# Linear attention and feed-forward in one kernel: rows in three half-batch slots, two normalisations on other engines, another order at the passage, and the state sums' bank for attended products

## What is computed

```python
q, k, v = x @ Wq.T + bq, x @ Wk.T + bk, x @ Wv.T + bv      # split in 16 heads of 16
q = softmax(q, axis=-1);  k = softmax(k, axis=-2)          # k over the rows
state = einsum('bhnd,bhne->bhde', k, v)
out = einsum('bhnd,bhde->bhne', q, state)
out = layer_norm(out) * ln_g + ln_b
x = layer_norm(x + out @ Wo.T + bo)                         # attention layer
h = gelu(layer_norm1(x) @ ternary(w1).T + b1)               # 1024 hidden
x = layer_norm(x + layer_norm2(h) @ ternary(w2).T + b2)     # feed-forward layer
```

## Time and profile before

| | us |
|---|---|
| median of 3 runs | 558.14 (557.33 to 558.61) |
| profiled execution | 558.38 |
| its span, first to last instruction | 556.4 |
| TensorE busy in the span | 533.2 (96%) |
| VectorE, ScalarE, GpSimd busy | 481.3, 481.7, 405.7 |
| TensorE's mean granted clock | 0.992 |

### The profile page before, as it was taken

The page is one execution under the profiler, slowest core; times in us unless marked ns, Lnnn a source line. Parts: engine busy times, 40 slices in busy tenths (PEclk is TensorE's granted clock), DMA queues, the critical chain, the costliest instruction groups (busy, mean ns, idle before and its releaser), DMA issues. The chain is left out here.

```text
span 556.4 us, 10878 instructions
## 1 busy us (share of the span) xinstructions
PE 533.2 (96%) x3533; PEld 490.5 (88%) x3533; DVE 481.3 (86%) x1230; ACT 481.7 (87%) x955; POOL 405.7 (73%) x420
## 2 busy tenths in 40 slices
PE   8999999999999999989899999999999999999991
PEld 7999999898999989779788998999999999999890
DVE  5878998989899898948687899999999999999895
ACT  5746798798979878778889999999999999999993
POOL 3965979877787977476558876876776776676693
PEclk9999999999999999999999999999999999999996
DMA  8530050411605030241111022222012222110012
GB/s 340 201 113 0 4 226 2 173 56 69 234 1 228 1 115 39 75 155 75 76 40 33 13 71 77 77 76 68 39 50 77 77 77 77 45 34 38 39 39 113
DMA packets 12679, 46.51 MB, mean 84 GB/s; under 512 B 1360, under 2 KB 3792, under 8 KB 10448
## 3 DMA queue, kind: packets, MB, share of 16 engines
q1 hardware_dynamic: 12336, 45.28, 22.6%
q10 hardware_dynamic: 288, 0.54, 0.3%
HBM read 29.01 MB, written 16.81 MB: 82 GB/s over the span
## 5 line engine op out<-in xcount | busy, mean ns | idle before, releaser
L1957 PE MATMUL qps_sps_aps_then_y<-ff_w_over_xc_lo,ff_a_lo_over_qw 128*128 128x258 f32 x512 | 126.7, 283 | 0.0
L1957 PE MATMUL qps_sps_aps_then_y<-ff_w_over_xc_lo,ff_a_hi_over_xc_lo 128*128 128x258 f32 x512 | 126.6, 283 | 0.0
L1308 DVE SCALAR_TENSOR_TENSOR ff_a_lo_over_qw<-ring,ff_rho,ff_a_hi_over_xc_lo 128x512 fp32r<-128x512 f32 x128 | 93.0, 745 | 15.5 <-ACT ff_a_hi_over_xc_lo L847 14.6
L1933 PE MATMUL ring<-ff_ht_hi_over_qw,t 128*128 128x512 f32 x256 | 104.0, 406 | 0.9 <-DVE ff_ht_lo_over_xc_hi L1300 0.5
L1933 PE MATMUL ring<-ff_ht_lo_over_xc_hi,t 128*128 128x512 f32 x256 | 100.7, 393 | 0.0
L1957 PEld LDWEIGHTS qps_sps_aps_then_y<-ff_w_over_xc_lo,ff_a_hi_over_xc_lo 128*128 128x128 f32 x512 | 96.9, 189 | 3.6
L1957 PEld LDWEIGHTS qps_sps_aps_then_y<-ff_w_over_xc_lo,ff_a_lo_over_qw 128*128 128x128 f32 x512 | 96.6, 189 | 3.4
L829 ACT ACTIVATE ring<-ring,bias 128x512 f32<-128x512 f32 x128 | 84.0, 685 | 7.8 <-PE ring L1933 6.8
L553 POOL TENSOR_TENSOR ff_accp_over_xt_lo<-ff_accp_over_xt_lo,ff_sq_over_ek_et_hi 128x512 f32<-128x512 f32 x66 | 86.1, 1304 | 2.9
L845 ACT ACTIVATE ff_sq_over_ek_et_hi<-ring 128x512 f32<-128x512 f32 x128 | 80.6, 630 | 0.5
L847 ACT CAST ff_a_hi_over_xc_lo<-ring 128x512 fp32r<-128x512 f32 x128 | 79.5, 621 | 0.0
(11 more groups left out here) (191 smaller groups left out, 1605.0 us busy)
## 6 DMA issues: line engine op xcount, KB each, us to landing
xt<-in_x_tok_dram SPq DMA_DIRECT2D x8, 1024.0 KB, 4.8
out_dram<-ff_z_over_et_lo SPq DMA_DIRECT2D x15, 512.0 KB, 3.2
x_scratch<-z SPq DMA_DIRECT2D x14, 514.0 KB, 3.1
ff_x_over_w_raw_xc<-x_scratch SPq DMA_DIRECT2D x14, 514.0 KB, 4.9
xc<-in_x_chan_dram SPq DMA_DIRECT2D x6, 1024.0 KB, 6.9
w_raw<-in_w_dram SPq DMA_DIRECT2D x2, 1024.0 KB, 6.0
ek<-in_x_chan_dram SPq DMA_DIRECT2D x1, 1024.0 KB, 8.1
x_scratch<-xt SPq DMA_DIRECT2D x2, 512.0 KB, 5.5
```

Source lines behind the costliest of these rows:

```text
L1308: nc.vector.scalar_tensor_tensor(out=ff_a_lo[:, m % DEPTH], in0=ff_bank(k, m), scalar=ff_rho[:, m:m + 1], in1=ff_a_hi[:, m % DEPTH].bitcas ...
L1933: mm = nc.tensor.matmul(ff_bank(k, m), t1[:, c, m * P:(m + 1) * P], h[:, k % 2, c], start=(c == 0 and j == 0), stop=(c == CH - 1 and j == 1))
L1957: last = nc.tensor.matmul(ff_yps[:, t, 0:C + 2], a[:, m % DEPTH, t * P:(t + 1) * P], ff_w2[:, m], start=(m == 0 and j == 0), stop=(m == FC ...
```

## The change

- `z` becomes three slots of four tiles (`z_slot`, `ZG` = 3), each with its own semaphore for the store. `product_out` waits at each half-batch for the store that used the slot three half-batches ago.
- `ATTEND_AT` uses all four banks in turn in the first six batches; `LAST_AT` uses banks 2, 3 and 1 in the last two. `attend` waits for q of b+2 at tiles 2 and 3 in place of 1 and 3. `state_sum(b, 0)` waits for six `product_out` of batch b-1.
- `normalise(5, 1)` becomes `early_normalise` on VectorE, in two pieces between statistics of batch 6. `normalise(6, 0)` and `(6, 1)` become `late_normalise` on GpSimd, behind `ff_keep_residual(0, 0)`. `norm_rstd` gets waits that guard its scales until these have read them.
- At the passage: on SyncE the first four feed-forward loads stand ahead of the stores of batches 5 and 6; on ScalarE, VectorE and TensorE steps change places as in the diff. `ff_split_gain` is cut in `gain_front` and `gain_back`, which move behind `residual(5, ...)` and behind the first statistics of batch 6.

The diff without most of its context; two hunks in which `z_rows(b)[:, t]` only becomes `z_tile(b, t)` are left out:

```diff
@@ -44,7 +44,8 @@
-ATTEND_AT = (2, 3, 2, 0, 3, 2, 0, 3)
+ATTEND_AT = (2, 1, 3, 0, 2, 1, 3, 0)
+LAST_AT = (2, 3, 1, 2, 3, 1, 2, 3)
@@ -83,6 +84,7 @@
     XB = 4
+    ZG = 3
@@ -108,7 +110,7 @@
         pt_hi, pt_lo = sb("pt_hi", [P, CH, N], F32R), sb("pt_lo", [P, CH, N], F32R)
-        z = sb("z", [P, T, C + 1])
+        z = sb("z", [P, ZG, GROUP, C + 1])
@@ -245,7 +247,8 @@
             sem(s) for s in ("z_ok", "z_mean", "z_sq", "z_var", "z_eps", "z_rstd", "z_fin", "x1_ok"))
-        x1_out = sem("x1_out")
+        x1_out = [sem(f"x1_out{n}") for n in range(ZG)]
+        x1_last_out, x1_early, x1_late = sem("x1_last_out"), sem("x1_early"), sem("x1_late")
@@ -279,8 +282,14 @@
-        def z_rows(b):
-            return z_last if b == NB - 1 else z[:, :, 0:C]
+        def z_slot(b, g):
+            return (NG * b + g) % ZG
+
+        def z_tile(b, t):
+            return z_last[:, t] if b == NB - 1 else z[:, z_slot(b, t // GROUP), t % GROUP, 0:C]
+
+        def z_stores(slot, groups):
+            return len([n for n in range(groups) if n % ZG == slot])
@@ -288,9 +297,11 @@
+        def attend_at(b):
+            return ATTEND_AT if b < NB - 2 else LAST_AT
+
         def a_bank(b, t):
-            n = ATTEND_AT[t] if b < NB - 2 else 2 + t % 2
-            return ff_yps[:, n]
+            return ff_yps[:, attend_at(b)[t]]
@@ -348,11 +359,22 @@
                     gs = slice(g * GROUP, (g + 1) * GROUP)
-                    sp.wait_ge(x1_ok, T * b + GROUP * (g + 1))
+                    if b < NB - 3 or (b == NB - 3 and g == 0):
+                        sp.wait_ge(x1_ok, T * b + GROUP * (g + 1))
+                    elif b == NB - 3:
+                        sp.wait_ge(x1_early, GROUP)
+                    elif b == NB - 2:
+                        sp.wait_ge(x1_late, GROUP * (g + 1))
+                    else:
+                        sp.wait_ge(x1_ok, T * (NB - 3) + GROUP * (g + 2))
                     if b < NB - 1:
-                        sp.dma_start(x1_scratch[b, :, gs], z[:, gs]).then_inc(x1_out, 16)
+                        sp.dma_start(x1_scratch[b, :, gs], z[:, z_slot(b, g)]).then_inc(x1_out[z_slot(b, g)], 16)
                     else:
-                        sp.dma_start(x1_scratch[b, :, gs, 0:C], z_last[:, gs]).then_inc(x1_out, 16)
+                        sp.dma_start(x1_scratch[b, :, gs, 0:C], z_last[:, gs]).then_inc(x1_last_out, 16)
+
+            def stored(groups):
+                for slot in range(ZG):
+                    sp.wait_ge(x1_out[slot], 16 * z_stores(slot, groups))
@@ -374,7 +396,7 @@
             sp.dma_start(rows[:, 1:], rows_d[:, 1:]).then_inc(rows_in, 16)
-            for b in range(NB):
+            for b in range(NB - 1):
@@ -385,15 +407,18 @@
                     sp.dma_start(f_raw, w1.rearrange("p a f -> p (a f)")).then_inc(f_in, 16)
-            sp.wait_ge(x1_out, 16 * NG * (NB - 2))
             sp.wait_ge(f_tern, 8)
             sp.wait_ge(xc_lo_ok, CH * (NB - 1))
+            stored(NG * XB // 2)
             for k in range(XB):
                 ff_load(k)
+            store(NB - 3)
             store(NB - 2)
+            stored(NG * (NB - 2))
             ff_load_over(XB)
             store(NB - 1)
-            sp.wait_ge(x1_out, 16 * NG * NB)
+            stored(NG * (NB - 1))
+            sp.wait_ge(x1_last_out, 16 * NG)
@@ -476,6 +501,10 @@
                 pool.wait_ge(z_eps, n)
+                if b == NB - 2 and g == 1:
+                    pool.wait_ge(x1_early, GROUP)
+                if b == NB - 1:
+                    pool.wait_ge(x1_late, GROUP * (g + 1))
@@ -483,8 +512,15 @@
                 pool.wait_ge(z_fin, 4 * n - 1)
-                var = last_var[:, gs] if b == NB - 1 else z[:, gs, C]
+                var = last_var[:, gs] if b == NB - 1 else z[:, z_slot(b, g), :, C]
                 nc.gpsimd.tensor_tensor(var, vaZ[:, gs], eps[:, gs], ALU.add).then_inc(z_fin, 1)
+
+            def late_normalise(g):
+                pool.wait_ge(z_fin, 4 * (NG * (NB - 2) + g + 1))
+                for t in range(g * GROUP, (g + 1) * GROUP):
+                    row = z_tile(NB - 2, t)
+                    nc.gpsimd.tensor_scalar(row, row, rsZ[:, t:t + 1], nmr[:, t:t + 1], ALU.mult, ALU.add
+                                            ).then_inc(x1_late, 1)
@@ -606,6 +642,8 @@
             ff_keep_residual(0, 0)
+            late_normalise(0)
+            late_normalise(1)
@@ -733,13 +771,13 @@
                     return
-                if t == 0:
-                    if b < NB - 1:
-                        wait_for(act, x1_out, 16 * NG * b)
-                    else:
-                        act.wait_ge(z_ok, T * b)
+                if t % GROUP == 0 and b < NB - 1:
+                    n = NG * b + t // GROUP
+                    wait_for(act, x1_out[n % ZG], 16 * (n // ZG))
+                elif t == 0:
+                    act.wait_ge(z_ok, T * b)
                 act.wait_ge(a_stat, T * b + t + 1)
-                nc.scalar.copy(z_rows(b)[:, t], a_bank(b, t)[:, P:P + C]).then_inc(y_out, 1)
+                nc.scalar.copy(z_tile(b, t), a_bank(b, t)[:, P:P + C]).then_inc(y_out, 1)
@@ -952,16 +990,15 @@
             squares(NB - 3, 0)
+            state_out(NB - 2)
             squares(NB - 3, 1)
-            state_out(NB - 2)
-            normalise(NB - 3, 0)
             k_exponent(NB - 1, 0)
             projected_high(NB - 2)
-            normalise(NB - 3, 1)
+            normalise(NB - 3, 0)
+            k_exponent(NB - 1, 1)
+            product_out(NB - 2, 0)
             tok_hi(NB - 1)
-            product_out(NB - 2, 0)
             product_out(NB - 2, 1)
-            k_exponent(NB - 1, 1)
@@ -985,15 +1022,13 @@
             state_copy(NB - 1)
+            ff_ht_high(0, 1)
             squares(NB - 2, 0)
-            ff_ht_high(0, 1)
             state_out(NB - 1)
+            ff_gelu(0, 0)
+            projected_high(NB - 1)
+            ff_gelu(0, 1)
             squares(NB - 2, 1)
-            normalise(NB - 2, 0)
-            projected_high(NB - 1)
-            ff_gelu(0, 0)
-            ff_gelu(0, 1)
-            normalise(NB - 2, 1)
@@ -1224,12 +1259,19 @@
                     nc.vector.scalar_tensor_tensor(
-                        out=z_rows(b)[:, t], in0=z_rows(b)[:, t], scalar=rsA[:, t:t + 1],
+                        out=z_tile(b, t), in0=z_tile(b, t), scalar=rsA[:, t:t + 1],
...
+            def early_normalise(ts):
+                dve.wait_ge(z_fin, 4 * NG * (NB - 2))
+                for t in ts:
+                    row = z_tile(NB - 3, t)
+                    nc.vector.tensor_scalar(row, row, rsZ[:, t:t + 1], nmr[:, t:t + 1], ALU.mult, ALU.add
+                                            ).then_inc(x1_early, 1)
+
@@ -1258,7 +1300,7 @@
-            def ff_split_gain():
+            def gain_front():
@@ -1268,6 +1310,8 @@
                 nc.vector.tensor_tensor(ff_g_all[:], ff_g_all[:], ff_flat[:], ALU.add).then_inc(ff_g_step, 1)
+
+            def gain_back():
@@ -1500,22 +1544,25 @@
                     split_vectors()
-                    ff_split_gain()
...
             e_inverse(NB - 2)
+            gain_front()
...
             projected(NB - 2)
+            q_inverse(NB - 1, 1)
+            folded_bias()
             projected_low(NB - 2)
-            folded_bias()
             k_maximum(NB - 1, 1)
+            product_stats(NB - 2, 0)
+            gain_back()
+            product_stats(NB - 2, 1)
             ff_sum_columns()
-            q_inverse(NB - 1, 1)
-            product_stats(NB - 2, 0)
-            product_stats(NB - 2, 1)
+            early_normalise((4, 5))
             product_stats(NB - 2, 2)
+            early_normalise((6, 7))
@@ -1533,16 +1580,16 @@
             out_variance(NB - 2, 1)
+            ff_ht_low(0, 0)
             residual(NB - 2, 0)
+            e_inverse(NB - 1)
+            ff_ht_low(0, 1)
+            state(NB - 1)
             residual(NB - 2, 1)
-            e_inverse(NB - 1)
-            state(NB - 1)
-            ff_ht_low(0, 0)
-            ff_ht_low(0, 1)
+            projected(NB - 1)
             ff_norm_apply(1, (0, 1))
-            projected(NB - 1)
+            projected_low(NB - 1)
             ff_norm_apply(1, (2, 3))
-            projected_low(NB - 1)
@@ -1790,9 +1837,9 @@
                     pe.wait_ge(pt_lo_ok, PAIRS * b + CH * (g + 1))
-                if t in (1, 3) and b + 2 < NB:
-                    pe.wait_ge(q_sub, PAIRS * (b + 2) + (3 if t == 1 else 4))
-                last_use = [n for n in range(t) if ATTEND_AT[n] == ATTEND_AT[t]] if b < NB - 2 else range(t - 1)
+                if t in (2, 3) and b + 2 < NB:
+                    pe.wait_ge(q_sub, PAIRS * (b + 2) + t + 1)
+                last_use = [n for n in range(t) if attend_at(b)[n] == attend_at(b)[t]]
@@ -1811,6 +1858,7 @@
                     wait_for(pe, m_cent, CH * b)
+                    wait_for(pe, y_out, T * (b - 1) + 6 if b else 0)
@@ -1949,8 +1997,6 @@
                             pe.wait_ge(f_out, 3)
```

(12 more changed lines are left out.)

4 lines of the change are left out of this document (2 added, 2 removed).

## The result

The changed kernel takes 560.63 us (560.57 to 561.63, five runs), the kernel before 558.14 (557.33 to 558.61): 1.0051 times as long, 95% interval 1.004 to 1.0062. The forecast was 555.0 us, with a range to 558.2. It is wrong in sign, by 5.6 us.

A forecast was written before the change was run, and what follows sets the result against it. The prediction held the kernel bound by TensorE's own instructions. It summed 5.7 us won and 2.5 lost, net 3.2: 558.38 to 555.2 us for a profiled execution, 555.0 for the median, range 552.5 to 558.2.

The forecast's parts named there:

- early_normalise: Four VectorE tensor_scalars between batch 6's statistics: no cost taken, some 0.3 us for a pair if cover is gone.
- late_normalise: GpSimd ahead of attention_rstd(7, 0): eight take 3.4 us, two residuals wait; net 1.4 us lost at ff_first(0, 5), bounds 0 and 2.5.
- Slots: Batch 6's attended products: ScalarE's 2.6 us store wait goes, and TensorE's stall at 246.34; gain 1.3 us.
- The 0.13 us that each stall was to give: Added to the gain for each TensorE stall removed, since the matmul that resumes takes longer; an estimate.
- The order in the first half: Passage's first half, normalising off ScalarE and steps reordered: stalls of 0.81 and 1.15 us go, gain 2.2 us.
- the chain of batch 7: Steps up to batch 7's attended products: 0.4 us gained at the wait for xe, 1.4 at the 272.04 stall.
- The new wait at the state sum: First state sum behind et_low(7, 0), VectorE waiting for GpSimd's scale: 1.0 us stall, 0.4 at next transposes; 1.4 lost.
- The loop: Four banks gain 0.3 us, state sums waiting for the sixth copy lose 0.6: net 0.3 us lost.
- C: Rival: each late_normalise instruction costs 1.0 us on GpSimd, in full at ff_first(0, 5): 559.6 us; chance 0.12.
- D: Rival: a late store holds the slots, the 246.34 stall moves to tile 4: 556.3 us; chance within the forecast's 0.48.
- A: Rival: the new waits at state sums and residual don't bite: 552.8 us, 553.5 if one half-bites; chance 0.22.
- B: Rival: ScalarE and VectorE limit the passage, gains are lost again at 286: about 557.6 us; chance 0.18.

The follow-up runs named there:

- experiment 2: Kernel after, with the four VectorE instructions of early_normalise in the accumulator form, sums unread: 558.28 us, ratio 1.0005 to the kernel before.
- Experiments 5 and 6: Kernel before plus eight unread GpSimd tensor_scalars where late_normalise stands in the kernel after: 558.06 us; with thirteen 559.14 us, with sixteen 561.25 us.
- early_accum: The kernel of experiment 2: kernel after, early_normalise's instructions also writing an unread sum, 558.28 us.
- experiments 7 and 8: Kernel after with all three normalisations on ScalarE: 555.17 us; with all three on GpSimd where it idles: 554.61 us, with old banks for batches 0 to 5 too 554.08.
- before_pool13: Kernel before plus thirteen unread GpSimd tensor_scalars ahead of attention_rstd(7, 0): 559.14 us, ratio 1.002.
- before_pool16: Kernel before plus sixteen unread GpSimd tensor_scalars ahead of attention_rstd(7, 0): 561.25 us, ratio 1.005.
- banks_old: Kernel after with the old banks for batches 0 to 5 and no wait of their state sums for the sixth copy: 560.83 us, ratio 1.0048.

## Why the prediction was wrong, step by step

**`early_normalise`: the step that failed first.** "I take nothing for it, and if that cover is gone some 0.3 us for a pair." The cover (statistics that wait for TensorE) was there, but the price of a pair was not 0.6 us: it was 2.80 and 2.50, as long as GpSimd's instruction beside it. By experiment 2, with the same work in a form that isn't shut out, it cost 2.35 us. I had looked at the shutting out for the residual, took it for a matter of instructions with two inputs, and did not ask it of a VectorE instruction with one input in the very stretch where I had GpSimd's 4.87 us on record.

The Trainium skill says more than I used of it (SBUF — State Buffer, Who interferes with whom): tensor_scalar, except in the form that also writes out its accumulator, can enter a mode that uses both read ports, and then excludes GpSimd, and is excluded, for the whole instruction; VectorE: DVE Perf Modes (Mode 2×_2P) gives the condition, one source, source and destination in SBUF. By that rule the traces agree as far as wide instructions of GpSimd go: 2.48 and 2.18 us for the two that met its low parts against 0.54 in the accumulator form, and 1.27 against 0.17 us for four columns beside a square sum of 512. They don't agree for GpSimd's instructions on four columns: in the 13 traces `ff_norm_apply`'s instruction began over 500 times while one that takes a power (1.0 to 1.1 us) was running, and it never took more than 0.36 us.

**`late_normalise`: the mechanism was right, the size was off.** The wait at `ff_first(0, 5)`, the scale and the clash of two residuals came as described, and the place was named as what would make the forecast wrong. Three terms were mis-sized. The eight took 4.34 us, not 3.4, 0.54 each: inside the bounds of 2.9 to 4.4, at the end that I did not take. The two residuals lost 0.84 + 1.01 us where 1.1 and 1.3 were expected, so this term was if anything too big; but the prediction took about 1.0 us off for slack (1.1 + 1.3 became 1.4), and there was none: all of 0.84 + 1.01 + 1.05 = 2.9 us arrived at TensorE, as 3.0. The third is the start: I moved ScalarE's squares of batch 6 behind r_hi and gelu and never followed GpSimd's chain that waits for them, so "the scale is then ready about when VectorE comes" was 1.05 us wrong. Experiments 5 and 6 show that it counts when they end, and with a given number when they start: eight at the earlier place cost nothing, and it takes more than eight there to bring the stall.

**The clock: not in the sum at all.** I had put it at nothing without a reason: I bounded the net loss at `ff_first(0, 5)` by 2.5 us and counted an idle microsecond as one. The idle time there was 3.5 us, and behind it TensorE had the lower clock for 3.4 us, which cost 1.54 us more. Neither end of the range had a place for that.

**What held.** Slots: the wait of 2.6 us for a store is gone and the stall at the third tile with it, though the clash hid the gain until experiment 2. How much that is differs between executions, since the stall was 0.36 to 1.34 us in the four traces of the kernel before and its variants. The 0.13 us that each stall was to give on top is a little high: in the trace before, a matmul that resumes behind a stall is 0.06 to 0.11 us longer than the median of its kind. The order in the first half and the chain of batch 7: the stalls went as forecast, and with the clash away the second row of the table is -4.45 us against the forecast's -3.9. The new wait at the state sum was there but smaller, 0.45 us against 1.0, and the next transposes had none. It shows (0.41 to 0.45 us) in early_accum and in the four kernels with `early_normalise` on GpSimd; in the kernel after TensorE came to the state sum too late to wait. The loop: +0.38 against +0.3, with the state sum of pass 3 at 126.52 behind the sixth copy as forecast; pass 6 is alike. SyncE's order cost nothing visible.

**The rivals.** C named the right place and came near the time, 559.6 us, but that is luck, for its price was not the measured one: an instruction of 0.54 us is far from the 0.82 where it decides. The net loss was a late start with two residuals held up, the clash of a different instruction 36 us earlier, and the clock. D fell: the stall at tile 5 of batch 6 looks like a slot that came late, but its releaser waited for VectorE's statistic, and not for a store. A fell as well. B, that the passage has no room for a gain, is refuted by experiments 7 and 8: 2.9 and 4.0 us are there.

What stays open: why the clock fell in some executions behind idles of 1.6 to 2.0 us and not in others; why before_pool13 has three long executions; and what lengthens the last stage by 0.3 us (219.61 to 219.69 against 219.32 to 219.40) in the four kernels that have `early_normalise` on VectorE, and in no other.

## What to carry to other kernels

Work taken from a busy engine must be priced beside what the receiving engine's neighbour does in that very stretch: a plain tensor_scalar on VectorE with operands in SBUF, be it on 256 columns or on four, was held until the tensor_tensor of GpSimd on 512 or 1024 columns beside it was over, while its form with an accumulator was not, and GpSimd's instructions on four columns did not hold it. When a step moves later on one engine, follow the chain that waits for it to the end before calling another engine's idle time a cover; the same eight instructions were free 2.2 us behind a landmark and cost 3.3 us, the clock's fall included, 6.4 behind it. And price a long idle of TensorE with the clock behind it.

## What the runs showed of the hardware that I had not expected

- Behind an idle of TensorE of 3.05 to 3.53 us the granted clock was at the lower level (0.50) for 3.4 us in the profiled executions of the kernel after, early_accum and before_pool16, and for 6.8 us in banks_old (in early_accum and banks_old it fell 0.13 and 1.45 us before the idle was over); the cost was 1.5 us for 3.4. Behind idles of 1.60 and 1.99 us it fell in two profiled executions, and behind 1.61, 1.63 and 1.64 us it stayed up.
- A form that does more work can be the faster one beside a busy GpSimd: 0.54 us for each of four tensor_scalars with an accumulator; without it 0.40 us for the two that were not held, and 2.18 and 2.48 for the two that were.
- GpSimd's tensor_tensors on 512 and 1024 columns held VectorE's plain tensor_scalar (1.27, 2.18, 2.48 us); those on four columns, of 1.0 to 1.1 us, did not (at most 0.36 us).
- GpSimd takes 0.54 us for a tensor_scalar on 128x256 in float32 (4.34 and 4.30 us for eight). The 0.72 us on 128x512 is 0.18 more for twice the width, so by these two sizes much of the price is fixed.
